# Sending x and the context to SBUF as 104 and 112 rows a transfer, and writing the zeros of the spare output rows after the biases

## What is computed

```python
def attention(query, key):
    a = jnp.einsum('bqd,bkd->bqk', query, key)
    e = jax.nn.softmax(a, axis=-1)
    return jnp.einsum('bqk,bkd->bqd', e, key)

def experts(x, W_gate, b_gate, W_e, b_e):
    _, top_idx = jax.lax.top_k(x @ W_gate + b_gate, 2)
    y_all = jax.nn.relu(jnp.einsum('bsd,edh->bseh', x, W_e) + b_e)
    return jnp.take_along_axis(y_all, top_idx[..., None], axis=2).mean(axis=2)

x = x + jnp.tanh(g_xattn[0]) * attention(layernorm(x), ctx)
x = x + jnp.tanh(g_ffn[0]) * experts(layernorm(x), W_gate, b_gate, W_e, b_e)
```

## Time and profile before

| | us |
|---|---|
| three executions | 342.31, 344.61, 344.61 |
| the profiled execution, its time | 344.43 |
| the profiled execution, its span | 342.3 |
| TensorE busy | 316.7 (93% of the span) |
| DVE, ACT, gpsimd busy | 203.3, 122.7, 76.4 |
| moved by DMA | 90.57 MB, 265 GB/s over the span |

### The profile page before, as it was taken

How to read it: one execution, slowest core, us unless ns; L and a number is a source line. 1 busy time by engine, 2 the same in 40 slices (tenths; PEclk the granted TensorE clock), 3 DMA queues, 4 the chain that set the end, 5 groups by cost and what they waited for, 6 DMA issues and landing times.

```text
span 342.3 us, 4344 instructions
## 1 busy us (share of the span) xinstructions
PE 316.7 (93%) x1510; PEld 233.4 (68%) x1510; DVE 203.3 (59%) x434; ACT 122.7 (36%) x165; POOL 76.4 (22%) x95
## 2 busy tenths in 40 slices
PE   5878799999999999969999999999999999999960
PEld 4533466565665588848887888888888888888850
DVE  2308258677668888954787766755176675753220
ACT  2403434625534558012544525515031551331000
POOL 6001111201203210311333521530121333111130
PEclk9999999999999999999999999999999999999995
DMA  7899999999958799769999999898469989644142
GB/s 222 330 276 306 362 284 369 335 315 381 388 199 294 247 401 332 211 212 274 333 314 358 352 359 342 225 386 264 61 184 349 267 216 389 198 61 65 11 80 31
DMA packets 25115, 90.57 MB, mean 265 GB/s; under 512 B 2912, under 2 KB 3936, under 8 KB 25084
## 3 DMA queue, kind: packets, MB, share of 16 engines
q1 hardware_dynamic: 15628, 57.19, 48.6%
q0 software_dynamic: 6320, 21.14, 24.7%
q10 hardware_dynamic: 3136, 11.83, 10.0%
HBM read 73.63 MB, written 16.52 MB: 263 GB/s over the span
## 4 chain that ended last, share of the span: by engine, by line
PE 67%; DMA 22%; DVE 4%; issue 2%; POOL 1%; SPq 1%; ACT 1%; POOLq 0%; DVEq 0%
PE ps L460 41%; PE ps L368 9%; PE ps L393 9%; DMA out_rows<-x_all 7%; DMA kT<-in_ctx_cols 6%; DMA out_rows<-y,dst_token 3%; DMA xg<-hn_rows,src_token 3%; PE ps L443 3%; DMA bias<-in_L_ffn_b_e 2%; PE ps L414 2%; PE ps L405 1%; PE ps L359 1%; DVE x_all L811 1%; DMA x_all<-in_x 1%; DVE stats L760 1%
## 5 line engine op out<-in xcount | busy, mean ns | idle before, releaser
L460 PE MATMUL ps<-wh,xh 128*128 128x512 f32 x256 | 82.9, 400 | 0.1
L460 PE MATMUL ps<-wl,xh 128*128 128x512 f32 x256 | 80.4, 393 | 0.3 <-issue 0.3
L460 PE MATMUL ps<-wh,xl 128*128 128x512 f32 x256 | 79.2, 393 | 0.0
L903 DVE TENSOR_TENSOR wl<-raw,wh 128x1024 fp32r<-128x1024 f32 x64 | 75.5, 1217 | 5.5 <-ACT wh L653 5.5
L653 ACT ACTIVATE wh<-raw 128x1024 fp32r<-128x1024 f32 x64 | 63.5, 1051 | 16.9 <-DMA raw<-in_L_ffn_W_e 14.8
L460 PEld LDWEIGHTS ps<-wl,xh 128*128 128x128 f32 x256 | 48.0, 188 | 11.4 <-issue 0.7
L460 PEld LDWEIGHTS ps<-wh,xl 128*128 128x128 f32 x256 | 47.9, 188 | 10.5
L460 PEld LDWEIGHTS ps<-wh,xh 128*128 128x128 f32 x256 | 46.5, 188 | 9.4 <-issue 0.5
L1085 POOL DMA_INDIRECT out_rows<-y,dst_token x15 | 29.5, 1966 | 101.8 <-DVE y L917 79.4
L656 ACT ACTIVATE xh<-ps 128x1024 fp32r<-128x1024 f32 x16 | 16.4, 1024 | 95.7 <-PE ps L443 95.7
L368 PE MATMUL ps<-kT,qT 128*100 128x361 f32 x128 | 41.2, 471 | 5.4 <-DMA kT<-in_ctx_cols 4.4
(11 more groups left out here) (122 smaller groups left out, 239.3 us busy)
## 6 DMA issues: line engine op xcount, KB each, us to landing
raw<-in_L_ffn_W_e SPq DMA_DIRECT2D x64, 512.0 KB, 9.9
kT<-in_ctx_cols SPq DMA_DIRECT2D x16, 722.0 KB, 14.4
ctx<-in_ctx ACTq DMA_DIRECT2D x8, 1024.0 KB, 12.4
bias<-in_L_ffn_b_e SPq DMA_DIRECT2D x8, 512.0 KB, 9.9
ctx<-in_ctx ACTq DMA_DIRECT2D x8, 420.0 KB, 15.4
hn_rows<-hn POOLq DMA_DIRECT2D x8, 384.0 KB, 7.3
out_rows<-x_all SPq DMA_DIRECT2D x1, 3072.0 KB
x_all<-in_x SPq DMA_DIRECT2D x7, 384.0 KB
```

What stands on the lines that cost most here:

```text
L460: mm = nc.tensor.matmul(into[:, n * HB:(n + 1) * HB], rows[:, k, :], weights[:, k, n * HB:(n + 1) * HB], start=(k == 0 and c == first), st ...
L903: nc.vector.tensor_tensor(wl[e % 2][:, k, :], raw[e % 2][:, k, :], wh[e % 2][:, k, :], ALU.subtract).then_inc(s_wl, 1)
```

## The change

x arrives in DRAM with 104 rows a batch and the context with 368; the added rows are zero. The turned context stays at 361 columns. x is loaded with one DMA of 104 partitions instead of two of 96 and 4, and its semaphores are waited for at 16. The last piece of the context is loaded as 112 partitions instead of 105. Everything that reads x_all reads its first 100 partitions, and TensorE reads 105 rows of the last context chunk as before. The stores of x_all and hn keep their 96 + 4 rows. The two zero writes move behind the biases of experts 0 and 1.

```diff
-    B, Q, D = x.shape
-    KV = ctx_rows.shape[1]
+    B, Q_LOAD, D = x.shape
+    Q = (out.shape[0] - 2 * P) // B
+    KV = ctx_cols.shape[3]
+    KV_LOAD = ctx_rows.shape[1]
...
-        stack3, (x_all,) = region([("x_all", [Q, B, D], F32)])
+        stack3, (x_all,) = region([("x_all", [Q_LOAD, B, D], F32)])
...
             def load_x(b):
-                for first, end in X_PARTS:
-                    sp.dma_start(x_all[first:end, b, :], x[b, first:end, :]).then_inc(s_x[b - 1], 16)
+                sp.dma_start(x_all[:, b, :], x[b, :, :]).then_inc(s_x[b - 1], 16)
...
             for h in range(2):
-                for first, end in X_PARTS:
-                    sp.dma_start(x_all[first:end, 0, h * 512:(h + 1) * 512], x[0, first:end, h * 512:(h + 1) * 512]
-                                 ).then_inc(s_x0[h], 16)
+                sp.dma_start(x_all[:, 0, h * 512:(h + 1) * 512], x[0, :, h * 512:(h + 1) * 512]).then_inc(s_x0[h], 16)
...
             for first, end in X_PARTS:
                 sp.dma_start(*hidden(first, end)).then_inc(s_hstore, 16)
+
+            sp.wait_ge(s_hn, B)
+            sp.wait_ge(s_hstore, 16 * len(X_PARTS))
+            load_bias(0)
+            load_bias(1)
+
             sp.wait_ge(s_const, 1)
             for t in range(HALVES):
                 rows = out[N_TOK + t * P:N_TOK + (t + 1) * P, :].rearrange("p (a d) -> p a d", d=256)
                 sp.dma_start(rows, zero[:, :].unsqueeze(1).to_broadcast([P, D // 256, 256])).then_inc(s_zero, 16)
-
-            sp.wait_ge(s_hn, B)
-            sp.wait_ge(s_hstore, 16 * len(X_PARTS))
-            load_bias(0)
-            load_bias(1)
...
             def load_values(b):
-                first, rows = KV_T[LAST]
+                first, _ = KV_T[LAST]
...
-                act.dma_start(ctx_t[b % 2][0:rows, LAST, :], ctx_rows[b, first:KV, :]).then_inc(s_ctx[b % 2][1], 16)
+                act.dma_start(ctx_t[b % 2][0:KV_LOAD - first, LAST, :], ctx_rows[b, first:KV_LOAD, :]
+                             ).then_inc(s_ctx[b % 2][1], 16)
...
-                    dve.wait_ge(s_x[b - 1], 32)
+                    dve.wait_ge(s_x[b - 1], 16)
...
-                        dve.wait_ge(s_x0[h], 32)
+                        dve.wait_ge(s_x0[h], 16)
...
-        give(name, a)
+        if name in ("x", "ctx_4096"):
+            give(name, np.pad(a, ((0, 0), (0, -a.shape[1] % 8), (0, 0))))
+        else:
+            give(name, a)
```

More of the change, by code:

```diff
@@ L610, in normalise @@
             def normalise(dst, b, column_no, done):
-                nc.scalar.activation(dst[:, :], x_all[:, b, :], ACT.Identity, bias=shift[:, column_no:column_no + 1],
+                nc.scalar.activation(dst[:, :], x_all[0:Q, b, :], ACT.Identity, bias=shift[:, column_no:column_no + 1],
                                      scale=inv_std[:, column_no:column_no + 1]).then_inc(done, 1)
@@ L758, in measure @@
             def measure(b, column_no, h):
-                nc_rows = x_all[:, b, h * 512:(h + 1) * 512]
+                nc_rows = x_all[0:Q, b, h * 512:(h + 1) * 512]
                 return nc.vector.bn_stats(stats[:, column_no, h, :], nc_rows)
@@ L809, in add_attention @@
                 dve.wait_ge(s_att, b + 1)
-                rows = x_all[:, b, :]
+                rows = x_all[0:Q, b, :]
                 nc.vector.scalar_tensor_tensor(out=rows, in0=att_ps, scalar=coef[:, 0:1], in1=rows,
```

## The result

| | median | from, to | executions |
|---|---|---|---|
| before | 343.15 us | 342.09 to 344.61 | 15 |
| after | 347.87 us | 343.71 to 351.26 | 15 |

The ratio of after to before is 1.0102, 95% interval 1.0074 to 1.0130. The forecast was 340.6 us with a range to 345.5. The kernel after scatters by 7.6 us here and the kernel before by 2.5; beside the experiments, with 23 to 35 executions, the kernel before scatters by 6.8 to 8.0 us in four of five series (the fifth has one execution of 1149 us), so the scatter is no mark of the change. The ratios here leave out the executions more than 1.5% above a kernel's fastest; where a kernel scatters wider than that, its median over all executions stands beside the ratio.

What follows compares the result with a forecast made beforehand. TensorE was taken to bound the kernel except in two holes, the load stage (waiting for keys) and tile 2 (waiting for its gather). 344.43 less 2.4 (loads) less 1.4 (zeros) gave 340.6 us, range 338.2 to 345.5.

Steps and rivals of the forecast that it cites:

- I charge the 3 us to them; that is the weakest step here.: Load stage: some rings run 3 us behind what their bytes explain, charged to the small DMAs of x's four-row tails.
- my sum: Load stage: rows per ring until batch 2's keys, at 299 GB/s; an even ring is through at 32.2 us.
- The first rival: Load stage: delay never the tails', so it gives nothing and the tail 1.4 us: 343.0 us; chance 0.23.
- SP issues two loads for batch 0 instead of four ..., which starts the queue that much earlier.: Start of SP's queue: two fewer x loads for batch 0 start the queue 0.77 us earlier.
- The bound of a loss, 0.2 to 1.0 us: Load stage: if the four rings are late for another reason, added rows cost 1.0 us, less 0.77 or nothing.
- The rings are 0.98 busy, so no ring idles.: Load stage, 10.0 to 36.1 us: argument for the rings staying late, as 299 GB/s may be all available.
- Granted clock ... drops out of the argument.: TensorE: granted clock is 1.00 in all four stretches read, the upper level, so it was left out.
- the 2.3 that I took: Tile 2's gather, after the x_all store: 2.3 us gained, bound 0 to 2.57, as rings go on to it, not zeros.
- 2.5 MB stand ahead of the last zero: Zeros behind the biases: that traffic at 299 GB/s takes 8.5 us, so the zeros land at 152.9 us.
- The third rival: Zeros cost by piece, landing at 160.8 us; first add 6.8 us late, whole 348.8 us; chance 0.10.
- the 1.4 us that I took: Tail: gain from moving the zeros behind the biases, 1.3 us through tile 5's gather plus 0.1 for a less crowded add.
- the four signs that I had named for a wrong forecast: scores(2) resumes at 36 or later; gpsimd zeros wait over 2 us; xg wait near 180 over 1.5; rings not 13.

Runs made afterwards that it cites:

- e3: Kernel before with x padded to 112 rows in one DMA on 16 rings, context 112, zeros ahead of the biases: 345.3 us, ratio 1.0050.
- e5: Kernel before with x's 104 rows as 96 + 8 in two DMAs, context 112, zeros ahead of the biases: 344.45 us, ratio 1.0042.
- e2: Kernel before with only the loads changed (x as one DMA of 104, context 112), zeros ahead of the biases: 350.2 us, ratio 1.0239.
- e8: Second run of the kernel before with only the loads changed (x as one DMA of 104, context 112): 348.87 us, ratio 1.0161.
- e18: Third run of the kernel before with only the loads changed (x as one DMA of 104, context 112): 349.39 us, ratio 1.0102.
- e9: Kernel before with x as 96 + 8 in two DMAs, context 112, zeros written before the weights of expert 1: 342.39 us, ratio 0.9959.
- e1: Kernel before with only the two zero writes moved behind the biases, all loads as before: 341.5 us, ratio 0.9981.
- e7: Kernel before with only the two zero writes issued early, ahead of the weights of expert 1: 340.4 us, ratio 0.9894.
- e17: Kernel before with batch 0's x as 52 + 52, later batches one DMA of 104, context 112, zeros ahead: 344.17 us, ratio 1.0035.

## Why the prediction was wrong

**"I charge the 3 us to them; that is the weakest step here."** This step failed. The tails carry no such delay: without any, on sixteen rings (e3), the last half of the keys of batch 2 lands at 35.88 us, where my sum gives 32.2 and before has 36.08, and the kernel is at 1.0050; with eight-row tails (e5) it is at 1.0042. So the change had no delay to take away. What it brought instead, one DMA on 13 rings for a load, has a price of its own, to which the sum gave no term: 4.7 to 7.4 us by the medians of e2, e8 and e18, most of it in the first loads. Instead of 2.4 us gained the load stage lost 3.9 in the profile of after. Why such loads slow the keys behind them stays open. The first rival, *the rings stay late*, had the premise right and the price wrong: it put the stage at nothing, and the whole at 343.0 us, measured 347.87.

**"SP issues two loads for batch 0 instead of four ..., which starts the queue that much earlier."** The issue is earlier, 2.52 and not 3.63 us, but I took an earlier issue for an earlier landing, and its sign was wrong: the second half of batch 0's keys lands at 14.15 us (2.52 + 11.63), and scores(0), which I had not looked at because nothing waited there, now wait. The bound of a loss, 0.2 to 1.0 us, was worked out from row counts alone; nothing in it could show a slower packet (331 ns for a piece of the keys, before 286).

**"The rings are 0.98 busy, so no ring idles."** That was a mean over 26 us. From 10 to 14 us the share of before is 0.71, in the rows above; the stage was not ring-bound from end to end.

**"Granted clock ... drops out of the argument."** It did in before. In after TensorE stands for 3.2 and 2.3 us and goes on at the lower level: scores(2) take 6.67 us for sixteen products, where in before the two groups of eight took 2.65 and 2.68:

```profile
31.52 2.65 PE L368 MATMUL ps<-kT,qT 128*100 128x361 f32 x8 [0.79 <-DMA kT<-in_ctx_cols]
36.12 2.68 PE L368 MATMUL ps<-kT,qT 128*100 128x361 f32 x8 [1.96 <-DMA kT<-in_ctx_cols]
```

By the Trainium skill (TensorE: Matmul & The Clock Gate, "Part 1: The HAM clock gate") activity is what releases the throttle; the trace agrees, 0.57 over 186 to 190 us after 0.36 us of work from 184 to 186, and 1.00 again from 190 to 195 after 4.00 us of work without a gap. The length of one stop does not foretell it here: after 1.64 us in e2 the clock fell (0.50 from 33.7 to 37 us), after 2.67 us in e9 and 2.26 in e8 it stayed at 1.00.

**The zeros.** The gather of tile 2 and y(0) came out as forecast: the hole is gone, and y(0) is ready 2.5 us later than in before (156.54 for 154.02) where the store started 5.0 us later, so 2.5 us were gained for the 2.3 that I took. What was mis-sized is the term "2.5 MB stand ahead of the last zero", 8.5 us. Packets of after from 148 to 160 us and their queues, then the packets from 148 to 153, from 153 to 158 and from 158 to 160 us:

```profile
DMA packets 1829, 3.88 MB, mean 324 GB/s; under 512 B 116, under 2 KB 1140, under 8 KB 1828
...
q1 hardware_dynamic: 1526, 2.79, 71.1%
q0 software_dynamic: 302, 1.07, 24.1%
```

```profile
DMA packets 328, 1.23 MB, mean 246 GB/s; under 512 B 27, under 2 KB 28, under 8 KB 328
...
DMA packets 1287, 1.92 MB, mean 385 GB/s; under 512 B 69, under 2 KB 1071, under 8 KB 1286
...
DMA packets 214, 0.73 MB, mean 365 GB/s; under 512 B 20, under 2 KB 41, under 8 KB 214
```

The 1024 packets of 1 KB are the zeros (1140 - 116), 1.05 MB. SP's queue moved 2.79 MB, so 1.74 MB more of its own passed before the last zero landed. The two biases are 1.05 MB together (128 x 4 KB each), so at least 0.7 MB of that are weights of expert 2, asked for behind the zeros; 1.07 MB are gathers. Three things in my term were off. In the first 5 us only one zero starts (28 - 27): the biases and gathers ahead pass at 246 GB/s, where I had 299. By 158 us 3.15 MB have passed, not 2.5, and 1003 of the zeros with them. And the last 21 zeros (41 - 20) start only in the 2 us behind that, beside 0.6 MB of weights asked for later; a sum over all rings at one mean rate has no place for the last ring. The third rival, "the zeros cost by piece and not by byte", named the place and the point from which it decides ("as soon as the zeros land after y(0)"), and its 15.0 us from issue to landing (145.8 to 160.8) lie nearer to 12.0 than my 7.1. Its reason is not what happened: in the trace a packet of 1 KB takes 46 ns and one of 4 KB 159 ns (medians, 148 to 160 us), so a piece of the zeros costs under a third of a row, not as much as one. I had given it 0.10. By e1 the part is worth 0.9981, not the 1.4 us that I took.

Of the four signs that I had named for a wrong forecast three came: scores(2) went on at 36.00 us ("36 or later", and there only with the first half), gpsimd waited 6.4 us for the zeros, TensorE 2.3 us for xg. The fourth, another number of rings than 13, did not.

The chances: "slower" had 0.10, most of it from late zeros and a little from a load stage that loses up to 1.0 us. No case held a load stage that loses more than 1.0 us, though the stage was the one place where I had no row for the delay that I explained.

## What to carry to other kernels

A delay that no row names must not be put down to the part that the change removes; give the opposite sign a price too. Before removing an issue at the start of a queue, look at what follows it closely, and at shares in slices of a few us, since a stage's mean hides both idle rings and slow packets. Fewer DMAs for the same rows are not cheaper by themselves; here one was dearer than two. A write that nobody needs for long is best issued where its queue stands still anyway and well ahead of the first wait for it (e7), because what is asked for behind it can pass first (at least 0.7 MB did here).

## What was not expected of the hardware

- The same 104 rows a load cost 4.7 to 7.4 us by the medians as one DMA on 13 rings and nothing that can be measured as 52 + 52 on 13 rings. Splitting the first two loads of the program alone gave back 5.2 us of the medians (e17 and e18).
- Keys asked for 1.1 us earlier (2.52, before 3.63) landed later: the rings moved 251 GB/s for 296 over 2 to 10 us at the same busy share (0.94), a piece of the keys took 367 ns for 286, and the rings that carry the second half of batch 0's keys finished up to 5.5 us apart (8.88 to 14.39 us in e18, before 9.82 to 11.43).
- A standstill of TensorE of 2 to 3 us can cost more than itself: in after the products behind it ran at a clock of 0.57 to 0.86 in the stretches above, and scores(2) took 1.3 us longer for it (6.67 against 5.33). It need not: in e8 and e9 the clock stayed at 1.00 after such stops.
